# A chunked linear attention: k turned through memory instead of on TensorE, y scaled by ScalarE, z in one instruction

## The reference

```
xn = layernorm(x);  q, k = rope(xn @ Wq.T), rope(xn @ Wk.T);  v = xn @ Wv.T;  gate = xn @ Wg.T
dt = softplus(xn @ Win.T + dt_bias);  G = cumsum of dt * -exp(A_log) in a chunk
scores = q k^T;  y = (scores * causal exp(G_i - G_j)) @ (v * dt)            # inside a chunk
cstate = (k * exp(Glast - G))^T @ (v * dt)                                  # of a chunk
state = state * exp(Glast) + cstate                                         # chunk after chunk
y = y + (q * exp(G)) @ state before the chunk
z = y / rms(y) * gnorm_w * gate * sigmoid(gate)
x = x + z @ Wo.T
x = x + (layernorm(x) @ W.T + b + a mixture of 8 rank-16 experts, weighted by a softmax)
```

## Time and profile before

| | |
|---|---|
| Median of 3 runs (lowest to highest) | 1765.15 us (1765.02 to 1765.41) |
| The profiled execution | 1765.26 us, span 1763.4 us from its first to its last instruction |
| Mean granted TensorE clock | 0.998 of full |
| TensorE / VectorE / GpSimd / ScalarE busy | 1738.6 / 1271.4 / 851.6 / 715.1 us |
| DMA | 190.31 MB, all work of one queue 35.6% of 16 engines |

### The profile page before, as it was taken

How to read it: one execution, slowest core, us unless ns; L and a number is a source line. 1 busy time by engine, 2 the same in 40 slices (tenths; PEclk the granted TensorE clock), 3 DMA queues, 4 the chain that set the end, 5 groups by cost and what they waited for, 6 DMA issues and landing times. The chain is left out here.

```text
span 1763.4 us, 27984 instructions
## 1 busy us (share of the span) xinstructions
PE 1738.6 (99%) x8744; PEld 1468.0 (83%) x8744; DVE 1271.4 (72%) x2353; ACT 715.1 (41%) x2232; POOL 851.6 (48%) x862
## 2 busy tenths in 40 slices
PE   7999999999999999999999999999999999999998
PEld 6788888888888888888888888888778888888886
DVE  5327899998989989889999998998864333333332
ACT  3424444444455444544445444544652212121111
POOL 3126676667667666767666666766401101010101
PEclk9999999999999999999999999999999999999999
DMA  6235323433433333332433333333572323232321
GB/s 208 91 100 146 91 73 118 116 93 112 120 87 118 118 86 111 114 102 77 118 117 90 111 120 88 118 88 105 195 253 76 99 78 102 76 103 74 104 73 47
DMA packets 145985, 190.31 MB, mean 108 GB/s; under 512 B 9136, under 2 KB 79792, under 8 KB 145840
## 3 DMA queue, kind: packets, MB, share of 16 engines
q1 hardware_dynamic: 145840, 188.58, 35.6%
HBM read 141.89 MB, written 46.66 MB: 107 GB/s over the span
## 5 line engine op out<-in xcount | busy, mean ns | idle before, releaser
L117 POOL TENSOR_TENSOR q<-raw_wo_early 128x512 f32<-128x512 f32 x128 | 165.3, 1291 | 195.8 <-DVE raw_wo_early L109 195.6
L88 PE MATMUL p_proj<-shared,wq_hi 128*128 128x512 f32 x744 | 244.5, 389 | 0.0
L1135 ACT ACTIVATE square<-p_y 128x128 f32<-128x128 f32 x512 | 134.2, 277 | 220.1 <-PE p_y L849 218.7
L1877 POOL TENSOR_TENSOR var<-mv,eps 128x1 f32<-128x1 f32 x16 | 3.0, 190 | 402.6 <-DVE mv L1727 402.6
L849 PE MATMUL p_y<-v_tok,probs 128*128 128x128 f32 x1024 | 183.0, 276 | 0.0
L1007 DVE SCALAR_TENSOR_TENSOR z<-p_y,srstd,gate 128x128 f32<-128x128 f32 x512 | 143.7, 343 | 51.6 <-issue 34.5
L1110 ACT ACTIVATE probs<-g_row,stab 128x128 f32<-128x128 f32 x512 | 164.3, 407 | 24.2 <-POOL g_row L1244 24.1
L88 PE MATMUL p_kept<-wg_hi,shared 128*128 128x512 f32 x560 | 173.1, 390 | 0.0
L1258 POOL TENSOR_TENSOR xw_lo<-xw_raw,xw_hi 128x512 fp32r<-128x512 f32 x96 | 131.0, 1364 | 86.0 <-ACT xw_hi L1151 86.0
L88 PEld LDWEIGHTS p_proj<-shared,wq_hi 128*128 128x128 f32 x744 | 139.7, 188 | 30.4 <-DVE raw_wo_early L109 1.2
L1266 POOL TENSOR_TENSOR srstd<-svar,mhalf 128x4 f32<-128x4 f32 x128 | 157.7, 1232 | 10.0
(11 more groups left out here) (244 smaller groups left out, 4395.3 us busy)
## 6 DMA issues: line engine op xcount, KB each, us to landing
g_row<-g_scratch SPq DMA_DIRECT2D x128, 256.0 KB, 5.1
z_scratch<-z_st SPq DMA_DIRECT2D x256, 128.0 KB
w_raw<-z_scratch SPq DMA_DIRECT2D x62, 512.0 KB, 6.7
e_row<-e_scratch SPq DMA_DIRECT2D x96, 256.0 KB, 4.1
w_raw<-in_wq_t SPq DMA_DIRECT2D x16, 512.0 KB, 7.3
w_raw<-in_wg_t SPq DMA_DIRECT2D x16, 512.0 KB, 5.6
v_tok<-v_scratch SPq DMA_DIRECT2D x32, 256.0 KB, 2.9
v_scratch<-n_xin SPq DMA_DIRECT2D x20, 256.0 KB, 2.3
```

The source lines that it names most:

```text
L88: mm = pe.matmul(out, lhs[a], rhs[e], start=(i == 0 and j == 0), stop=(i == len(pairs) - 1 and j == 2))
L117: pool.tensor_tensor(out, keep["rope_a"][:, s, :], keep["rope_b"][:, s, :], ALU.add).then_inc(keep["roped"], 1)
L1135: s = act.activation(square[:, h, :], p_y[c % 2][:, h, :], ACT.Square, scale=2.0 / float(np.sqrt(D)), accum_out=ssum[:, c, h:h + 1])
```

## The change

- `k_turn` stays for the first step alone (`first_k_turn`). Otherwise VectorE's `turn_k` turns the 32x32 blocks of k (one instruction of 128x384, behind `turn_z(n, 0)`), SyncE's `store_k` writes them in four DMAs to the place that they have in the turned matrix (pieces of 32 f32), and `load_turned` reads it back to `k_turned` in SBUF. `store_k` stands at c = 1 behind `load_e(g, b, 3)` and ahead of the weights of the next group, `load_turned` at c = 2 behind the g rows. ScalarE's `save_k` is renamed `k_tok_high`; it and `k_tok_low` read `k_turned` (`by_tokens`).
- ScalarE's `scale_y` multiplies y by `srstd` from PSUM into `z`, in four activations; `make_z` is one multiplication of `z` by the gate. `mix` waits for `y_scaled` instead of `z_set`. `scale_y(n, 2)` stands ahead of `q_high(n + 1, 0)`.
- ScalarE copies a step's first state (`save_first_state`).
- tanh is written to `gate` itself. VectorE rotates a unit first and makes z behind it. Some semaphores are merged.

```
+            def store_k(n):
+                sp.wait_ge(k_blocks_set, n)
+                for a in range(P // BL):
+                    sp.dma_start(k_dram.rearrange("c (b j) d -> j (c b) d", j=BL)[:, :, a * BL:(a + 1) * BL],
+                                 k_blocks[a * BL:(a + 1) * BL].rearrange("j c b i -> j (c b) i")).then_inc(k_out, 16)
+            def load_turned(n):
+                sp.wait_ge(k_out, 16 * (P // BL) * n)
+                sp.dma_start(k_turned[:, :, :], k_dram.rearrange("c t d -> t c d")).then_inc(k_in, 16)
...
                     elif c == 1:
                         sp.wait_ge(state_set, 3 * n + 2)
                         load_e(g, b, 3)
+                        if ahead(n):
+                            store_k(n + 1)
                     elif c == 2 and ahead(n):
+                        load_turned(n + 1)
                         sp.wait_ge(state_set, 3 * n + 3)
...
             def mix(g, b, n, c):
-                wait_ge(pe, z_set, m - 1)
+                wait_ge(pe, y_scaled, m - 1)
...
                 gates(g, b, n, 3)
-                k_turn(n + 1, b + 1)
                 mix(g, b, n, 3)
...
             def k_tok_low(n):
-                dve.tensor_tensor(k_tok[1][:, :, :], p_tok[:, 0:NC - 1, :], k_tok[0][:, :, :].bitcast(F32),
+                dve.tensor_tensor(k_tok[1][:, :, :], by_tokens(n), k_tok[0][:, :, :].bitcast(F32),
+            def turn_k(n, b):
+                dve.wait_ge(roped, ROPED * n + 1)
+                wait_ge(dve, k_out, 16 * (P // BL) * (n - 1))
+                dve.transpose(k_blocks[:, :, :, :], k[:, b % 2, 0:(NC - 1) * C].rearrange("p (c b i) -> p c b i", c=NC - 1, i=BL)
+                              ).then_inc(k_blocks_set, 1)
...
             def make_state(n, b, c):
-                if c == 0:
-                    s = dve.tensor_copy(state[:, 1, :, :], p_cst[:, :, :])
...
             def make_z(n, c):
-                dve.wait_ge(srstd_set, m + 1)
-                wait_ge(dve, turned, m)
-                for h in range(HG):
-                    zz = dve.scalar_tensor_tensor(z[:, h, :], p_y[c % 2][:, h, :], srstd[:, c, h:h + 1],
-                                                  gate[:, c % 2, h * D:(h + 1) * D], ALU.mult, ALU.mult)
-                zz.then_inc(z_set, 1)
+                dve.wait_ge(y_scaled, m + 1)
+                dve.tensor_tensor(z[:, :, :], z[:, :, :], gate[:, c % 2, :].rearrange("p (h d) -> p h d", h=HG),
+                                  ALU.mult).then_inc(z_set, 1)
...
                 make_probs(n, 0)
                 q_low(n, b, 1)
+                rotate_next(g, b, n, K_UNIT, 0)
                 if has_last(n):
                     make_z(n - 1, 3)
                     turn_z(n - 1, 3)
-                rotate_next(g, b, n, K_UNIT, 0)
-                make_state(n, b, 0)
...
+                rotate_next(g, b, n, Q_UNIT[1], 2)
                 make_z(n, 0)
-                rotate_next(g, b, n, Q_UNIT[1], 2)
                 turn_z(n, 0)
+                turn_k(n + 1, b + 1)
                 make_state(n, b, 1)
...
             def make_tanh(g, b, n, c):
-                wait_ge(act, gate_set, NC * n + c)
+                wait_ge(act, z_set, NC * n + c - 1)
...
+            def scale_y(n, c):
+                m = NC * n + c
+                act.wait_ge(srstd_set, m + 1)
+                wait_ge(act, turned, m)
+                for h in range(HG):
+                    y = act.activation(z[:, h, :], p_y[c % 2][:, h, :], ACT.Copy, scale=srstd[:, c, h:h + 1])
+                y.then_inc(y_scaled, 1)
+            def save_first_state(n):
+                act.wait_ge(cst_done, 3 * n + 1)
+                act.activation(state[:, 1, :, :], p_cst[:, :, :], ACT.Copy).then_inc(state_set, 1)
...
                 make_decay(n, b, 1)
+                if has_last(n):
+                    scale_y(n - 1, 3)
                 xw_high(n, 1)
+                save_first_state(n)
...
                 make_decay(n, b, 2)
+                scale_y(n, 0)
                 xw_high(n, 2)
...
                 make_decay(n, b, 3)
+                scale_y(n, 1)
 
                 squares(n, 2)
...
                 make_tanh(g, b, n, 2)
+                scale_y(n, 2)
                 if ahead(n):
                     q_high(n + 1, b + 1, 0)
                     if group_ahead(g) and b == B - 2:
...
```

More of the change, by code:

```diff
@@ L548, in attention_stage @@
         k_tok = [sb(f"k_tok_{e}", [P, NC - 1, D], F32R) for e in ("hi", "lo")]
+        k_blocks, k_turned = sb("k_blocks", [P, NC - 1, TB, BL]), sb("k_turned", [P, NC - 1, D])
+        k_dram = keep["k_dram"]
         stab = sb("stab", [P, 2, NC, TAB, HG])
@@ L643, in group_ahead, with by_tokens @@
             return not (isinstance(g, int) and g == KVH - 1)
+        def by_tokens(n):
+            return k_turned[:, :, :] if has_last(n) else p_tok[:, 0:NC - 1, :]
         def v_loads(g, b):
@@ L872, in first_heads @@
             def first_heads(n, s, j, some):
[L874 to L876 removed]
+                if s:
                     taken(n - 1, GATE_UNIT[3])
@@ L992, in make_state @@
                 dve.wait_ge(cst_done, 3 * n + c + 1)
-                if c == 0:
-                    s = dve.tensor_copy(state[:, 1, :, :], p_cst[:, :, :])
-                else:
-                    for h in range(HG):
-                        s = dve.scalar_tensor_tensor(state[:, (c + 1) % 2, h, :], state[:, c % 2, h, :],
-                                                     e_row[:, e_slot(b, c), h, C - 1:C], p_cst[:, h, :], ALU.mult, ALU.add)
+                dve.wait_ge(state_set, 3 * n + c)
+                for h in range(HG):
+                    s = dve.scalar_tensor_tensor(state[:, (c + 1) % 2, h, :], state[:, c % 2, h, :],
+                                                 e_row[:, e_slot(b, c), h, C - 1:C], p_cst[:, h, :], ALU.mult, ALU.add)
                 s.then_inc(state_set, 1)
@@ L1137, in squares, with k_tok_high @@
                 s.then_inc(squares_set, 1)
-            def save_k(n):
-                act.wait_ge(tok_done, n + 1)
-                wait_ge(act, cst_done, 3 * n)
-                act.activation(k_tok[0][:, :, :], p_tok[:, 0:NC - 1, :], ACT.Copy).then_inc(tok_hi_set, 1)
+            def k_tok_high(n):
+                if has_last(n):
+                    act.wait_ge(k_in, 16 * n)
+                else:
+                    act.wait_ge(tok_done, 1)
+                wait_ge(act, cst_done, 3 * n)
+                act.activation(k_tok[0][:, :, :], by_tokens(n), ACT.Copy).then_inc(tok_hi_set, 1)
+            def scale_y(n, c):
+                m = NC * n + c
+                act.wait_ge(srstd_set, m + 1)
+                wait_ge(act, turned, m)
+                for h in range(HG):
+                    y = act.activation(z[:, h, :], p_y[c % 2][:, h, :], ACT.Copy, scale=srstd[:, c, h:h + 1])
[3 more added lines that the diff above has]
+                act.activation(state[:, 1, :, :], p_cst[:, :, :], ACT.Copy).then_inc(state_set, 1)
             def save_last(i, bank_):
@@ L1171, in last_step @@
                         make_decay(n, b, c + 1)
+                    scale_y(*((n, c - 1) if c else (n - 1, 3)))
+                    if c == 0:
+                        save_first_state(n)
                     make_tanh(g, b, n, c)
@@ L1226, in _ @@
             squares(LAST, 3)
+            scale_y(LAST, 3)
             for at in range(8, SPLIT_EARLY):
```

69 lines of the change are left out of this document (34 added, 35 removed).

## The result

| | before | after |
|---|---|---|
| Median (lowest to highest, runs) | 1765.79 us (1765.02 to 1767.60, 6) | 1776.09 us (1772.71 to 1778.61, 6) |
| Profiled execution | 1765.26, span 1763.4 | 1776.84, span 1774.7 |
| Mean granted TensorE clock | 0.998 | 0.997 |

The change makes the kernel slower by 10.3 us: ratio 1.0056, 95% interval 1.0043 to 1.0069. Forecast were 1774.0 us, 1760 to 1784, slower as the likeliest.

A forecast was written before the change was run, and what follows sets the result against it. The prediction took TensorE's queue of matmuls to bound the attention stage. Span 1763.4 - 9.9 (transposes) + 12.6 (b = 2) + 6.3 (b = 3) = 1772.4 us, forecast as 1774 us measured, range 1760 to 1784.

The forecast's parts named there:

- TensorE's queue bounds the stage: Attention stage: an unbroken queue of matmuls, so work taken out of it shortens the run by its full issue time.
- The transposes give 31 x 0.32 = 9.9 us: Between last gate matmul and mix: all steps but the last lose k's three transposes, 0.32 us each, 9.9 us gained.
- VectorE's relief is worth 0: VectorE ends with some 2 us less per step, worth 0 by itself since it bounds nothing.
- scale_y takes 1.25 us for four: ScalarE's four activations for each chunk take 1.25 us, like the decay's 1.28, with a lower bound of 1.0.
- Ordinary steps have a margin of 0.2 us: At a step's end q_lo is ready 0.2 us before the scores need it, release included: no stall.
- b = 2, 7 x 1.8 = 12.6 us: End of steps b = 2: VectorE and GpSimd take turns, the state matmul stalls 1.8 us, seven times.
- b = 3, 7 x 0.9 = 6.3 us: Steps b = 3: k's stores delay the g rows, making srstd and the scores 0.9 us late, seven times.
- rival 4: Late in all steps: z waits for GpSimd's add, 30 x 0.5 = 15 us on top, 1789; chance 0.10.
- 1770 to 1782 by its bounds: Total time with both the b = 2 and b = 3 stalls, by the bounds of their sizes; chance 0.50.
- Signs: TensorE idle some 19 us, GpSimd's g waits above 10 us, p_score waiting for q_lo at ends of steps b = 3.

The follow-up runs named there:

- mixed-order kernel: The changed kernel with z again made from PSUM without scale_y, VectorE's half of wq earlier, rotations ahead of z only in steps b = 0: 1756.12 us.
- experiment 4: The kernel before with k's transposes left out for all steps but the first: 1760.80 us.
- experiment 2: The changed kernel with the old way of y (no scale_y, z in four instructions from PSUM), k still through memory: 1764.30 us.
- experiment 3: The changed kernel with k turned by TensorE again, scale_y and the single z instruction kept: 1775.82 us.
- Experiment 5: VectorE's half of the wq split moved to right behind k_low, on the kernel of experiment 2 (1759.61 us) and on that of experiment 1 (1763.07 us).
- experiment 7: k's stores moved behind the g rows and load_turned behind load_e, on the kernel of experiment 6 (1772.69 us) and on the changed kernel (1778.41 us).
- experiment 6: The changed kernel with GpSimd's subtractions of half of wq and wg cut to 16 of 512 columns: 1769.37 us.
- experiment 1: The changed kernel with scale_y(n, 2) moved behind q_high(n + 1, 0): 1767.39 us.

## Why the prediction held, and where it didn't

- *TensorE's queue bounds the stage.* Right. In the mixed-order kernel, with no wait left, every step is as long as its matmuls.
- *The transposes give 31 x 0.32 = 9.9 us.* 0.35 each, 10.9. But that is what they give only if nothing else is just in time: 5.0 in experiment 4.
- *VectorE's relief is worth 0.* Right, and the relief was smaller than "some 2 us per step": 0.5, because the single z and k_tok_lo wait for GpSimd. The fastest kernel has the four z instructions.
- *scale_y takes 1.25 us for four.* 1.14 (146.1 / 128), between the bound 1.0 and the value taken.
- *Ordinary steps have a margin of 0.2 us.* No stall, as forecast: b = 1 and b = 2 take 35.55. But the 0.2 for a release, read from xw_lo in the kernel before, was not one. TensorE had no wait there; where it waits for xw_lo, the matmul starts 0.05 to 0.06 behind its end (experiments 2 to 4), and the scores start 0.16 behind q_lo's (607.69 to 607.85). Most of the 0.2 was slack.
- *b = 2, 7 x 1.8 = 12.6 us.* Measured 7 x 1.86 = 13.0 (it shows in the next step's period). GpSimd's wq_lo was forecast at 0.1 us before to 0.2 behind the start of the scores and came 0.03 before. Experiment 5 shows that the turns are the cause of most of it: moving one instruction took away 4.3 and 4.7 us. The Trainium skill (SBUF — State Buffer, Who interferes with whom) adds that the order of issue decides who blocks. The traces agree for large instructions, in both orders (z and the add in steps 12 and 13, the two halves of wq in the changed kernel and in experiment 2), and not for small ones: in experiment 5 with the new y the moved wq_lo of step 10, issued 0.39 behind a 128x4 pow of GpSimd, ran in its bare 1.21, and the pow took 1.35 instead of 1.02.
- *b = 3, 7 x 0.9 = 6.3 us, from k's stores.* This is the step of the prediction that failed: the term stands in steps where it costs nothing. The delay exists: the four stores took 1.95 us to issue in step 11 (1.5 forecast; that a missing register saves time is shown by no row), the waits for g at the table rose from 10.5 to 27.5 us in total, and experiments 6 and 7 show it costing 0.2 to 1.4 us a step, and going with the stores, once nothing covers it. But in the changed kernel the b = 2 chain had made the matmuls late by 1.8, more than the delay, and I added two delays of one step that in fact overlap. In its place the steps b = 0 lost 6 x 1.02, and one more 1.12, 7.2 us together. That is rival 4's mechanism: a z that loses its turn to GpSimd's add. I had set it aside with "z is next in VectorE's queue and goes first", which holds in b = 1, 2 and 3. In b = 0 z came some 0.1 us later and lost its turn, and in four kernels this separates the 19 steps that stall from the 9 that do not (experiment 7). That the subtraction of wg and the g row together make z late is read from the order of the instructions; neither was taken away alone. The sum came out within 2.1 us of the median by luck: the misplaced term has nearly the right size.
- *1770 to 1782 by its bounds.* The bounds as stated, 1.45 to 2.0 us and 0 to 2 us, seven times each, give 1765 to 1783.
- *Signs.* Idle time 18.9 for some 19: right. g waits above 10 us was no sign, since they were 10.5 before. p_score waits for q_lo at the ends of steps b = 0, not b = 3.

## What to carry to other kernels

Work taken out of the bounding engine's queue also takes cover from every chain beside it: before counting the gain, look for each chain that ends within it, also those that the change doesn't touch. An instruction that waits for a late result belongs behind those in its queue that don't need it, however short it is. Where two engines exclude each other for whole instructions, ask for each pair that meets which is issued first and by how much: here 0.1 us decided over 1.0. Two delays of one step don't add up if the first one moves the deadline of the second.

## What the runs showed of the hardware

- The same VectorE subtraction of 128x1024 took 1.21 us alone and 3.42 behind one of GpSimd's (experiments 5 and 1). GpSimd's took 2.37 when it was issued first and 3.39 when it was issued second (experiment 2). Small instructions take part as well: GpSimd's 128x4 pow took 1.01 to 1.03 us where VectorE had nothing with two SBUF inputs beside it, and mostly 1.34 to 1.58 where it had (steps 5 to 16).
- Four 128x128 activations from PSUM with a per-partition factor took 1.14 us, where the decay of the same shape from SBUF takes 1.28.
- The step with a late p_cst was 0.1 us longer than the matmul was late (1.86 against 1.76): the matmuls at 539.12, 539.43 and 539.66 follow each other at 0.31 and 0.23, those at 593.81, 594.04 and 594.27, without a wait, at 0.23 each.
- Stores of k in pieces of 128 bytes, 48 KB each, landed 2.6 us after their issue at the median. With k's way the queue moved 200.78 MB at a share of 39.5% of 16 engines, before 188.58 MB at 35.6%. By an estimate from these, a megabyte of k's way kept the DMA engines busy 1.8 times as long as the average megabyte before.
